# Reordering the last additions of an attention and mixture-of-experts kernel between VectorE and GpSimd

## The reference, cut to what matters

```python
xn = _layernorm(x, axis=-1)
s = _L0_attn_ref(xn, Wq, Wk, Wv, Wo)
# ffn: 16 experts of width 176, the best 2 of each token, plus shared experts of twice that width
g = _silu(_L0_ffn_ref(xn, gate_w, w_gate_up, w_down, shared_gate_up, shared_down))
out = x + s * g
```

## Time and profile before

| | us |
|---|---|
| median of 3 runs | 672.02 |
| the runs | 671.1, 672.02, 673.05 |
| time of the profiled execution | 668.7 |
| its span, first to last instruction | 666.4 |
| VectorE's last instruction ends | 661.93 |
| busy: TensorE, VectorE, GpSimd, ScalarE | 642.0, 539.7, 480.5, 466.9 |

### The profile page before, as it was taken

The page is one execution under the profiler, slowest core; times in us unless marked ns, Lnnn a source line. Parts: engine busy times, 40 slices in busy tenths (PEclk is TensorE's granted clock), DMA queues, the critical chain, the costliest instruction groups (busy, mean ns, idle before and its releaser), DMA issues.

```text
span 666.4 us, 15689 instructions
## 1 busy us (share of the span) xinstructions
PE 642.0 (96%) x5124; PEld 465.0 (70%) x5187; DVE 539.7 (81%) x1628; ACT 466.9 (70%) x1253; POOL 480.5 (72%) x562
## 2 busy tenths in 40 slices
PE   8989999999999999999999999999999999999994
PEld 6656676767777676767776776777777777777772
DVE  5999999999999999999999999999984454333356
ACT  5599897877686766767676767768787855555542
POOL 4898879687667676687887878776769954555544
PEclk9999999999999999999999999999999999999998
DMA  9980002011600000001000101000054726786874
GB/s 299 346 253 1 1 1 33 11 24 32 164 1 1 1 1 1 1 25 35 25 24 24 40 8 40 9 33 1 9 96 118 213 37 127 144 154 146 218 266 158
DMA packets 70816, 52.11 MB, mean 78 GB/s; under 512 B 41376, under 2 KB 64128, under 8 KB 70752
## 3 DMA queue, kind: packets, MB, share of 16 engines
q1 hardware_dynamic: 66688, 40.83, 23.3%
q0 software_dynamic: 3792, 10.43, 5.3%
q10 hardware_dynamic: 272, 0.02, 0.0%
HBM read 24.75 MB, written 18.77 MB: 65 GB/s over the span
## 4 chain that ended last, share of the span: by engine, by line
PE 73%; DVE 11%; ACT 7%; issue 4%; POOL 3%; DMA 1%; DVEq 0%; ACTq 0%; POOLq 0%
PE bank L1652 12%; PE bank L1590 12%; PE bank L1669 10%; PE bank L1799 9%; PE bank L1621 9%; PE bank L1636 7%; PE bank L1833 6%; PE bank L1605 2%; DVE arena L1317 2%; PE bank L1808 2%; ACT arena L954 2%; DVE arena L1290 2%; DVE arena L1289 1%; PE bank L1530 1%; ACT arena L962 1%
## 5 line engine op out<-in xcount | busy, mean ns | idle before, releaser
L954 ACT ACTIVATE arena<-bank,nmax 128x448 f32<-128x448 f32 (+7 forms) x256 | 125.8, 507 | 36.6 <-DVE nmax L1305 36.2
L653 POOL TENSOR_TENSOR arena<-arena,rinv 128x64 f32<-128x64 f32 (+2 forms) x192 | 102.2, 561 | 65.1 <-DVE rinv L1311 64.9
L968 ACT CAST arena<-bank 128x512 f16<-128x512 f32 (+1 forms) x192 | 94.6, 524 | 38.6 <-PE bank L1636 37.7
L1590 PE MATMUL bank<-xnT_both,arena 128*128 128x512 f16 (+2 forms) x435 | 114.5, 379 | 5.7 <-DVE arena L1290 1.8
L1305 DVE CUSTOM_DVE_ANT_0 bank<-bank,mask_b 128x448 f32<-128x448 f32 (+7 forms) x256 | 109.5, 485 | 7.2 <-issue 7.1
L1652 PE MATMUL bank<-arena 128*128 128x512 f16 (+7 forms) x751 | 113.9, 297 | 1.1 <-DVE arena L1322 0.2
L1317 DVE TENSOR_TENSOR arena<-bank,arena 128x512 bf16<-128x512 f32 (+1 forms) x192 | 108.7, 594 | 4.3 <-ACT arena L968 3.6
L641 POOL TENSOR_TENSOR arena<-arena 128x512 f32<-128x512 f32 x79 | 100.8, 1276 | 12.0 <-DVE s_sb L1333 8.5
L1621 PE MATMUL bank<-arena 128*128 128x448 bf16 (+3 forms) x767 | 104.6, 286 | 2.3 <-POOL arena L646 1.2
L646 POOL TENSOR_TENSOR arena<-arena 128x512 bf16<-128x512 f32 x80 | 92.6, 1167 | 16.8 <-ACT arena L942 16.7
L1636 PE MATMUL bank<-ident_f,arena 128*128 128x128 f32 x640 | 94.1, 275 | 3.5 <-DVE arena L1317 2.5
(11 more groups left out here) (167 smaller groups left out, 1110.4 us busy)
## 6 DMA issues: line engine op xcount, KB each, us to landing
stage<-w_gate_up SPq DMA_DIRECT2D x16, 352.0 KB
xs_dram<-compare SPq DMA_DIRECT2D x3, 1560.0 KB, 15.8
arena<-ys_dram SPq DMA_DIRECT2D x8, 512.0 KB, 7.9
stage<-w_down SPq DMA_DIRECT2D x16, 176.0 KB
stage<-wq SPq DMA_DIRECT2D x4, 512.0 KB, 9.6
stage<-wo SPq DMA_DIRECT2D x4, 512.0 KB, 8.4
stage<-x SPq DMA_DIRECT2D x1, 2048.0 KB, 13.2
out<-s_sb SPq DMA_DIRECT2D x7, 256.0 KB, 2.1
```

Source lines behind the costliest of these rows:

```text
L653: ins = pool.tensor_tensor(pr, pr, rinv[:, par, qt:qt + 1].to_broadcast([P, n]), ALU.mult)
L954: ins = act.activation(probs[par][:, P_AT[qt]:P_AT[qt] + n], score_bank[u][:, col:col + n], ACT.Exp, scale=-1.0, bias=nmax[:, par, qt:qt + ...
L968: act.copy(pT[j % 2][0][:, at:at + cols], pt_bank[(3 * j + u) % 2][:, 0:cols]).then_inc(pt_hi, 1)
L1590: ins = pe.matmul(ps[:], w[a][:, c * chunk:c * chunk + DH], tokens[m][:, c * TOK:c * TOK + S], start=(c == 0 and n == 0), stop=(c == KC - ...
```

## The change

The third early part's sum moves from the drain to the end of step -3, behind product 0. Inside a step the product now comes ahead of the sums. Product 2 is taken right behind the low halves of step 0, ahead of sums 3 and 4, which both stand in step 0. ScalarE's gate 2 moves from step 1 to step 0, gate 3 from behind the steps into step 1. x 5 moves from VectorE to the end of GpSimd's queue, and SP's write 5 waits for GpSimd's semaphore instead of VectorE's.

VectorE's order from step -3 was: hid, product 0; (-2) hid, low halves, product 1; (-1) hid; (0) low halves, sum 2; (1) sum 3; then sum 4, products 2 to 6, x 5, x 6, product 7, x 7, product 8, x 8. It becomes: hid, product 0, sum 2; hid, low halves, product 1; hid; low halves, product 2, sum 3, sum 4; then products 3 to 6, x 6, product 7, x 7, product 8, x 8.

```diff
-END_SUMS = {-5: 0, -4: 1, 0: 2, 1: 3}
-END_PRODUCTS = {-3: 0, -2: 1}
-END_GATES = {-4: 0, -3: 1, 1: 2}
+END_SUMS = {-5: [0], -4: [1], -3: [2], 0: [3, 4]}
+END_PRODUCTS = {-3: 0, -2: 1, 0: 2}
+END_GATES = {-4: 0, -3: 1, 0: 2, 1: 3}
...
             for g, t in enumerate(PARTS):
-                if g < EARLY_GROUPS:
+                if g <= EARLY_GROUPS:
                     sp.wait_ge(summed, g + 1)
                 else:
-                    sp.wait_ge(late_out, g - EARLY_GROUPS + 1)
+                    sp.wait_ge(late_out, g - EARLY_GROUPS)
...
-            for g in range(EARLY_GROUPS):
+            for g in range(EARLY_GROUPS + 1):
                 add_x(g)
...
             def end_parts(n):
-                if n in END_SUMS:
-                    add_shared(END_SUMS[n])
                 if n in END_PRODUCTS:
                     multiply(END_PRODUCTS[n])
+                for g in END_SUMS.get(n, []):
+                    add_shared(g)
...
             ffn_steps(step)
-            add_shared(EARLY_GROUPS - 1)
             for g in range(len(END_PRODUCTS), EARLY_GROUPS):
                 multiply(g)
             multiply(EARLY_GROUPS)
             multiply(EARLY_GROUPS + 1)
-            add_x(EARLY_GROUPS)
             add_x(EARLY_GROUPS + 1)
```

## The result

| | us |
|---|---|
| before, median of 22 runs | 672.96 |
| changed, median of 22 runs | 674.57 (672.95 to 677.64) |
| ratio | 1.0026, 95% interval 1.0018 to 1.0034 |
| profiled execution of the changed kernel | 675.93, span 674.1 |

A forecast was written before the change was run, and what follows sets the result against it. It took the start of the last writes' stream to bound the end; that stream ending at 664.17 instead of 663.65 gave +0.5 us, so 672.5 us against the median of 672.02, range 670.7 to 674.2.

The forecast's parts named there:

- What bounds the end: End of the launch: hangs on when the last writes' stream can start, not on VectorE's last instruction; 2.75 us follow it.
- the stream of the writes: Writes 5 to 8 at the end: starts 0.93 us after write 5's issue, takes 2.28, ends at 664.17, +0.5 us.
- x 5 on GpSimd: Last additions: saves VectorE 0.60, but x 5 waits for x 6, ends at 660.91; write 5 goes at 660.96.
- Two additions exclude each other for a whole instruction: VectorE and GpSimd additions from SBUF: the one that waited ends 0.55 (VectorE) or 1.12 us (GpSimd) after the other.
- Sum 2 in the wait: Step -3, behind product 0: pair 3 on GpSimd holds sum 2 until 649.72; `hid` of step -1 is 0.38 us late.
- slack of 1.4: Step -3: pair 2 is over at 646.74, 1.4 us before product 0 ends at 648.14, so sum 2 needn't wait for data.
- slower rival: Step -3: read-back for sum 2 3.4 us late or more, loss above 2.0 us, 674.1 and up; chance 0.06.
- Product 2 and sums 3 and 4: Step 0: product 2 starts at 653.13, x 2 then holds sum 4 until 656.08, a new collision costing 1.07 us.

The follow-up runs named there:

- late_memset: The kernel before with one memset of one number per partition added at the end of GpSimd's queue, behind product 8: 1.0025 of before, 1.8 us slower.
- sums_early_x34: The kernel before with sum 2 in step -3, sum 3 in step -1, x 3 and x 4 on VectorE: 0.9962 of before, 2.4 us faster.
- changed_again: The changed kernel measured once more, with nothing altered, beside three other experiments: 1.0033 of before, 2.3 us slower.
- sum2_later: The changed kernel with sum 2 at the end of step -1 instead of step -3: 1.0008 of before, 0.6 us slower.
- x5_back: The changed kernel with x 5 on VectorE again and write 5 behind VectorE's semaphore: 0.9985 of before, 0.8 us faster.
- changed_x45_back: The changed kernel with x 4 and x 5 on VectorE: 0.9974 of before, 1.7 us faster.
- x5_alone: The kernel before with x 5 alone moved from VectorE to the end of GpSimd's queue: 1.0008 of before, 0.3 us slower.

## Why the prediction was wrong, point by point

**What bounds the end: wrong, and this is the failed step.** The prediction first set VectorE's end aside, and rightly. Then it took the stream of the writes for the bound, "the end hangs on ... when the stream of the last writes can start", with 2.75 us from its end to the end of the span as a fixed rest. That rest was no rest: 2.1 of it was SP waiting for GpSimd's drain. It came from reading the chain of waits and the engines' timelines, which both end at 661.93, and never asking what the 4.5 us behind them hold. The prediction had the right number in its hands: x 5 on GpSimd ends at 660.91 against x 4's 659.65, 1.26 later. With 6.55 for the drain and the 0.55 of the changed kernel that is a span of 668.0, +1.6 us, and 1.7 (1.2 to 2.3) was measured. Part of that agreement is luck: the extra 0.3 behind the drain was in no row of before, and in the changed kernel's profile x 5 ends 2.1 later than before's x 4, as pair 2 was late. late_memset moves GpSimd's last end by 1.78 and, as far as its profile shows, nothing else, and costs 1.8. The stream of the writes was read rightly as far as it goes: with write 5 issued at 666.99 in the changed kernel, 0.93 and 2.28 more give 670.2, the DMA engines' share falls to 0.20 in the stretch from 670 to 671, and SP is ready at 670.8. It isn't what the launch waits for. That the forecast had the direction right comes from x 5, whose later end moves both the stream and the drain.

**Two additions exclude each other for a whole instruction: right**, and the sizes too. In the changed kernel x 2 ends at 661.56 and sum 4 at 662.12, 0.56 behind; x 5 ends at 666.96, 1.13 behind x 6. The page of the Trainium skill, "SBUF — State Buffer", section "A bandwidth-pool intuition that's wrong", has a blocked instruction run until the other's end plus about 115 ns, measured there on transfers whose descriptors GpSimd writes. These rows show no such surplus for two additions, like those of before: 0.56 is no more than the 0.60 between two free additions of VectorE, and 1.13 no more than the 1.2 between two of GpSimd.

**Sum 2 in the wait: right in kind, wrong in its spread.** +0.38 on `hid` of step -1 rested on pair 3 starting 0.44 behind product 0, which was rare: in the seven other profiles without a late read-back it starts between -0.39 and 0.03, and in the three of them that have sum 2 in step -3 it passes with 0.91 to 1.25 and `hid` at most 0.13 late. And in 6 of the 14 profiles pair 2 starts around product 0 (-0.07 to 0.98) instead of 2.0 to 2.3 ahead, for a read-back that lands some 2 us later. Where sum 2 stands in step -3 it then waits and is blocked as well, and `hid` is 1.4 and 1.5 late in the two profiles of the changed kernel and 1.8 in sums_early_x34. Such a lateness is beyond the slack of 1.4 that the prediction worked out. Its slower rival named this mechanism and asked for 3.4 or more, which no profile shows; the forecast itself took pair 2 to be in time, and it isn't in 6 of these 14 launches. The lateness may not be blind chance: SP issued the third read-back 7.5 to 7.9 us ahead of product 0 in the six, and 8.0 to 8.7 ahead in seven of the other eight (before, at 7.6, is the exception). No run moved the issue by itself, so what delays it stays open. In changed_again there is a further price, which the prediction didn't consider: TensorE, idle for 1.16 us and then 0.34, ran at a clock of 0.56 to 0.58 from 652 to 656, and its rows of part 5 took 3.43 for 1.88. The idle time alone doesn't account for that: in sums_early_x34 it was 1.46 and 0.34, and the clock stayed at 1.00. The rows of changed_again:

```profile
651.19 0.50 PE L1831 MATMUL bank<-shared_hi,arena 128*128 128x256 f16 x3 [1.16 <-DVE arena L1503]
...
652.56 3.43 PE L1849 MATMUL bank<-arena,ident_f 128*128 128x512 f32 x4
...
652.00:654.00 2.00, 1.97 (x5) 1.20 (x6) 0.63 (x3) 1.04 (x3) 1.93 (x2) 0.56 0.25 90
```

How much of the 1.6 us is due to the late read-backs can't be split off by these runs. With sum 2 moved out of their way (sum2_later) the loss is 0.6, so some 1.0 of it needs sum 2 in step -3. With x 5 taken back and sum 2 left there (x5_back) the kernel is 0.8 us faster than before, so all of it needs x 5 on GpSimd. Both work through the same term, the end of GpSimd's last instruction: 14.27 in the changed kernel, 13.06 in sum2_later, 11.39 in x5_back, 12.19 before.

**Product 2 and sums 3 and 4: right.** x 2 takes 1.65 and sum 4 1.76 (1.65 and 1.75 were named). Taken alone this is a loss of 1.1 us on VectorE, and it doesn't matter, since x 2 and with it GpSimd's queue start early: changed_x45_back is 1.7 us faster than before with the collision in it.

**x 5 on GpSimd: right in its times, 1.72 for the addition and the write right behind it; wrong in what it is worth.** Not the later write 5 was to be feared, but the last of GpSimd's instructions. x5_alone has SP ready 0.24 later than before and the span 1.34 later.

**Why the original idea lost.** It took VectorE, occupied to 661.93, for the bound and gave GpSimd one addition more. GpSimd carries 6.55 us behind its last instruction, so giving it less is the gain: with x 4 on VectorE instead of GpSimd the kernel is 1.9 us faster than before, with x 3 too, and sums 2 and 3 or sum 2 alone earlier, 2.4 and 2.5.

## What to carry to other kernels

Before anything at the end of a kernel is moved, read what lies between the last instruction of each engine and the end of the span, down to the drains in the queues: the engine that stops last isn't the one that ends the launch if another's drain is longer. In this kernel GpSimd's last instruction should end 6.55 us before the last write has landed, which is some 4.6 us before VectorE's last addition ends, since SP had seen the last write land 1.9 to 2.0 us behind that addition in nine of the fourteen profiles (2.4 to 2.7 in the others). And an instruction queued ahead of work on the critical path should wait for no transfer whose landing has only been seen in one profile; here one profile showed one landing out of a spread of some two us.

## What the runs showed of the hardware

- GpSimd's drain at the end of the program is over 6.55 us after its last addition in 13 profiles of 13, and 6.54 after a last memset in one; in before VectorE's takes 0.44, ScalarE's 0.40, and TensorE's 4.30 from 653.5, hidden there.
- A read-back of 512 KB, issued as third of eight in a row, let its pair start in two places, 2.0 to 2.3 us ahead of product 0 in eight profiles and around or behind it (-0.07 to 0.98) in six; in the six its landing came 3.4 to 4.5 us after the second one's, in the eight 1.4 to 2.8.
- TensorE's clock fell to 0.50 (1.2 GHz) within an idle time of 3.10 us in one profile and to 0.56 in the mean of two us behind idle times of 1.16 and 0.34 in another (changed_again), while idle times of 1.46 and 0.34 left it at 1.00 (2.4 GHz) in the profile of sums_early_x34, and 1.02 and 0.34 in that of the changed kernel.
